# Sparse graph attention: queries and residual rows of all targets in natural order beside the sort, with one gather per tile

## What is computed

```python
hs = layer_norm(x) * ln1_scale + ln1_bias          # sources
ht = layer_norm(h_target) * ln1_scale + ln1_bias   # targets
q, k, v = (ht @ Wq + bq) / sqrt(32), hs @ Wk + bk, hs @ Wv + bv
probs = softmax(where(adj != 0, q @ k.T, -1e30))   # per head
ht = ht + (probs @ v) @ Wo + bo
h2 = layer_norm(ht) * ln2_scale + ln2_bias
out = layer_norm(x + nodemask * (h2 + gelu(h2 @ W1) @ W2))
```

## Time and profile before

| what | value |
|---|---|
| median of the runs | 298.78 us (298.43 to 299.57, 3 runs) |
| span of the profiled execution | 290.6 us |
| time of that execution itself | not shown; the median is 8.2 us over the span |
| PE, VectorE, ACT, POOL busy | 226.5, 211.9, 165.7, 183.8 us |
| moved by DMA | 58.03 MB, 200 GB/s in the mean |

### The profile page before, as it was taken

The page is one execution under the profiler, slowest core; times in us unless marked ns, Lnnn a source line. Parts: engine busy times, 40 slices in busy tenths (PEclk is TensorE's granted clock), DMA queues, the critical chain, the costliest instruction groups (busy, mean ns, idle before and its releaser), DMA issues.

```text
span 290.6 us, 4144 instructions
## 1 busy us (share of the span) xinstructions
PE 226.5 (78%) x1319; PEld 177.8 (61%) x1319; DVE 211.9 (73%) x619; ACT 165.7 (57%) x286; POOL 183.8 (63%) x203
## 2 busy tenths in 40 slices
PE   7499998921124867899889898997799999597990
PEld 7344442300012555898779778996688898496990
DVE  2436999799843885696887869899979997798111
ACT  2598999800003467866866799686376534353420
POOL 8761536860048768787877867878856678047542
PEclk9789999995555699999999999999979999999997
DMA  6999999999975436655555645455662446112120
GB/s 167 357 399 415 417 410 416 406 396 333 365 228 175 147 103 189 187 166 157 153 169 165 177 123 161 136 169 173 187 167 77 121 138 151 38 38 72 36 72 27
DMA packets 23457, 58.03 MB, mean 200 GB/s; under 512 B 4019, under 2 KB 12485, under 8 KB 21382
## 3 DMA queue, kind: packets, MB, share of 16 engines
q0 software_dynamic: 8368, 27.01, 31.8%
q1 hardware_dynamic: 14228, 29.91, 27.3%
q10 hardware_dynamic: 834, 0.79, 1.3%
HBM read 51.40 MB, written 10.49 MB: 213 GB/s over the span
## 4 chain that ended last, share of the span: by engine, by line
POOL 26%; PE 20%; DVE 19%; issue 12%; DMA 11%; ACT 10%; SPq 1%; POOLq 0%; ACTq 0%; DVEq 0%
POOL arena L761 16%; DMA tab_scratch<-in_x_dram 6%; PE bank L1014 6%; PE bank L869 5%; POOL tab L751 4%; PE score L1005 4%; DVE arena L1699 4%; ACT arena L1210 4%; POOL rstd_late L781 4%; DVE arena L1705 3%; DMA arena<-kv_scratch,places 3%; ACT arena L1201 2%; ACT tab L1193 2%; DMA tab<-in_x_dram 2%; DVE arena L1658 2%
## 5 line engine op out<-in xcount | busy, mean ns | idle before, releaser
L761 POOL DMA_INDIRECT arena<-kv_scratch,places x79 | 87.9, 1112 | 22.2 <-issue 22.2
L1005 PE MATMUL score<-h_t,w_sb 128*128 128x128 f32 x512 | 62.3, 275 | 0.0
L1014 PE MATMUL bank<-w_sb,gelu_t 128*128 128x256 f32 x256 | 61.7, 386 | 0.0
L1005 PEld LDWEIGHTS score<-h_t,w_sb 128*128 128x128 f32 x512 | 60.0, 192 | 0.6 <-ACT h_t L1329 0.3
L1014 PEld LDWEIGHTS bank<-w_sb,gelu_t 128*128 128x128 f32 x256 | 47.8, 193 | 5.8
L1275 ACT ACTIVATE gelu_t<-score 128x512 f32<-128x512 f32 x32 | 19.1, 597 | 26.6 <-PE score L1005 26.4
L781 POOL TENSOR_TENSOR rstd_late<-var_late,minus_half 128x1 f32<-128x1 f32 (+3 forms) x23 | 21.0, 912 | 20.7 <-DVE var_late L1768 20.4
L751 POOL DMA_INDIRECT tab<-tab_scratch,places x16 | 17.7, 1109 | 22.5 <-DVE place_value L1628 18.1
L869 PE MATMUL bank<-tab,arena 128*128 128x512 f32 x64 | 30.7, 629 | 1.0 <-ACT arena L1201 0.7
L1658 DVE TENSOR_TENSOR arena<-arena,query 128x1024 f32<-128x1024 f32 (+3 forms) x22 | 24.5, 1113 | 4.4 <-DMA arena<-kv_scratch,places 2.3
L1660 DVE TENSOR_REDUCE logits<-arena 128x32 f32<-128x1024 f32 (+3 forms) x22 | 24.4, 1110 | 0.8
(11 more groups left out here) (148 smaller groups left out, 422.8 us busy)
## 6 DMA issues: line engine op xcount, KB each, us to landing
arena<-in_adj_dram SPq DMA_DIRECT2D x6, 1024.0 KB, 11.4
w_sb<-in_adj_dram SPq DMA_DIRECT2D x6, 1024.0 KB, 12.8
kv_scratch<-arena SPq DMA_DIRECT2D x8, 512.0 KB, 10.3
tab<-in_x_dram SPq DMA_DIRECT2D x4, 512.0 KB, 10.9
own_t<-in_adj_dram SPq DMA_DIRECT2D x2, 1024.0 KB, 11.1
gelu_t<-in_adj_dram SPq DMA_DIRECT2D x2, 1024.0 KB, 10.7
tab_scratch<-in_L_gnn_h_target_dram SPq DMA_DIRECT2D x1, 2048.0 KB, 13.0
tab_scratch<-in_x_dram SPq DMA_DIRECT2D x1, 2048.0 KB, 17.4
```

Of the source, the lines that this page charges most:

```text
L761: pool.indirect_dma_start(kv_ring[:, ring_at[m] + j, :], None, kv_dram[:, :], at).then_inc(gathered[m][piece], 16)
L1005: mm = pe.matmul(hid_ps[(2 * n + half) % 3][:, f % 4 * P:(f % 4 + 1) * P], w1_sb[:, k, f * P:(f + 1) * P], h2_t[:, n % 2, k, :], start=(k ...
L1014: pe.matmul(ff_ps[:, 0:D], gelu_t[:, n % 2, f, :], w2_sb[:, f, :], start=(f == 0), stop=False, skip_group_check=True)
```

## The change

The 2048 targets are treated like the sources, in natural order and before the sort has ended. h_target comes in four chunks of 512 rows (`load_h`) and runs through `unit_stats`, `rsqrt1`, a `normalise` that is now on POOL for chunks 2 to 7 (the last two of x, all of h), `turn_rows` and `copy_turned`. `project_target` makes the queries, `copy_target` takes them out, and `make_residual` on POOL makes the residual row (scale, shift and bo added). `save_table` stores both beside a copy of x in a table of 3 KB rows. After the sort one gather per tile brings x, residual and query; `turn_own`, `project_query`, `normalise_own`, `copy_own`, `copy_query`, the own statistics and `newton` are gone. `project_out` adds the gathered residual with one matmul by the identity. Wq's scaling goes from VectorE to POOL, the hidden layer gets a fourth PSUM bank, `WARM` grows from 32 to 72, and the orders of all engines are written anew. In the diff, parts for the dense path and declarations are left out.

```diff
-    TAB = 2 * D
+    TAB = 3 * D
+    Q_AT = 2 * D
...
+    OWN_AT = [3, 6, 10, 14, 18, 23, 28, 33, 39, 46, 54]
+    ROWS_BY = [(0, 7), (7, 13), (13, 20), (20, 26), (26, 34), (34, 41), (41, 48), (48, 55), (55, 61), (61, 68), (68, 75), (75, 81), (81, 81), (81, 81), (81, 81), (81, 81), (81, 81)]
...
-    WARM = 32
+    WARM = 72
...
+        lead_fetches = [(0, -1), (0, 0), (0, 1), (1, -1), (1, 0), (1, 1), (2, -1), (2, 0), (2, 1), (3, -1), (3, 0), (ROOT, "res"), (3, 1), (3, 2), (4, -1)]
...
+            def save_table(j):
+                sp.wait_ge(query_ready, j + 2)
+                sp.wait_ge(residual_ready, j // CT + 1)
+                sp.dma_start(tab_dram[j * P:(j + 2) * P, D:TAB].rearrange("(i p) n -> p i n", p=P),
+                             table_out[:, j:j + 2, :]).then_inc(table_saved, 16)
...
+            for t in range(0, 12, 2):
+                save_kv(t)
+            sp.dma_start(tab_dram[:, 0:D], x[:, :]).then_inc(rows_copied, 16)
+            save_kv(12)
+            save_kv(14)
+            for j in range(0, TILES, 2):
+                save_table(j)
...
+            def normalise(c):
+                pool.wait_ge(rstd_ready, turn_of[c] + 1)
+                for i in range(CT):
+                    rows = chunk_rows[c][:, i, :]
+                    pool.tensor_scalar(rows, rows, rstd[:, c, i:i + 1], shift[:, c, i:i + 1], ALU.mult,
+                                       ALU.add).then_inc(late_normed, 1)
+            def make_residual(c):
...
+                pool.tensor_tensor(rows, rows, scale_bc.rearrange("p (a n) -> p a n", a=1).to_broadcast([P, CT, D]),
+                                   ALU.mult).then_inc(residual_step, 1)
...
+                pool.wait_ge(coded, QK * (QUARTERS - 1 if k < CHUNKS // 2 else QUARTERS))
+                pool.tensor_tensor(made, rows, shift_bc.rearrange("p (a n) -> p a n", a=1).to_broadcast([P, CT, D]),
+                                   ALU.add).then_inc(residual_ready, 1)
...
             rsqrt1(2)
+            normalise(2)
             rsqrt1(3)
+            normalise(3)
+            pool.tensor_scalar(wq_sb[:, :, :], wq_sb[:, :, :], Q_SCALE, None, ALU.mult).then_inc(wq_scaled, 1)
+            rsqrt1(4)
+            normalise(4)
...
+            rsqrt1(5)
+            normalise(5)
             add_v(0)
-            wait_listing(0)
+            rsqrt1(6)
+            rsqrt1(7)
...
+            normalise(6)
+            normalise(7)
             add_v(1)
...
+            make_residual(4)
             add_v(2)
+            make_residual(5)
             add_v(3)
+            make_residual(6)
+            make_residual(7)
...
                     if m == 0:
-                        pool.wait_ge(rows_copied, 32)
+                        pool.wait_ge(rows_copied, 16)
+                        pool.wait_ge(table_saved, 16 * TILES // 2)
...
+            def project_target(j):
...
+                pe.matmul(proj_ps[t % 2][:, 0:D], ones_bf[:, :], bias_rows[:, :], start=True, stop=False, skip_group_check=True)
+                for k in range(DK):
+                    mm = pe.matmul(proj_ps[t % 2][:, 0:D], rows[:, k, :], wq_sb[:, k, :], start=False, stop=(k == DK - 1),
+                                   skip_group_check=True)
...
+            turn_rows(4)
             make_keys(2)
             project(13)
             project(14)
             project(15)
+            turn_rows(5)
+            project_target(0)
+            project_target(1)
             make_keys(3)
-            project_mean()
+            project_target(2)
+            project_target(3)
+            turn_rows(6)
+            project_target(4)
+            project_target(5)
+            project_target(6)
+            project_target(7)
+            turn_rows(7)
...
             pe.matmul(rank_ps[:, 0:P], class_total[:, :], below[:, :], start=False, stop=True).then_inc(rank_summed, 1)
+            project_target(8)
+            project_mean()
+            for j in range(9, TILES):
+                project_target(j)
...
+                pe.matmul(attn_ps[:, 0:D], ident[:, :], tab_of(n)[:, D:Q_AT], start=True, stop=False, skip_group_check=True)
...
+                for s in range(lo, hi):
+                    if s + 1 < hi:
+                        project_out(s + 1)
+                    mlp_in(s, 0)
+                    mlp_in(s, 1)
+                    mlp_out(s, 0)
+                    if s + 1 < hi:
+                        turn_h2(s + 1)
+                    if lo == 0 and s + 2 < hi:
+                        turn_context(s + 2)
+                    mlp_out(s, 1)
+                    add_h2(s)
...
+                weigh_keys(0, 0, SLOTS[ORDER[0]])
                 sum_tally()
                 weigh_values(0, 0, SLOTS[ORDER[0]])
                 weigh_keys(1, 0, SLOTS[ORDER[1]])
+                take_stats((0, -1), 0, None)
                 set_flag()
                 weigh_values(1, 0, SLOTS[ORDER[1]])
+                make_shift((0, -1))
                 weigh_keys(2, 0, SLOTS[ORDER[2]])
```

559 lines of the change are left out of this document (209 added, 350 removed).

## The result

| | before | after |
|---|---|---|
| median of the runs (lowest to highest) | 298.61 us (297.06 to 299.57) | 322.41 us (320.34 to 326.5) |
| ratio, 95% interval | | 1.0788 [1.0722, 1.0854] |
| span of the profiled execution | 290.6 | 318.6 |
| its own time | not shown | 320.34 |
| first gather F | 82.64 | 104.48 |

A forecast was written before the change was run, and what follows sets the result against it. The loop was taken as bound by PE's matmuls and, close by, POOL's gathers. First gather 14.4 us later, less 7.2 gained from there on, gave +7.2 on 298.8: 306.0 us, range 292 to 317.

The forecast's parts named there:

- What bounds the kernel: Loop: PE's matmuls and POOL's gather stream are two close bounds; the change lightens only the first, 95 gathers stay.
- room: End of the sort: only VectorE works (22.9 of 25.3 us), PE, ACT and POOL idle; not empty for transfers.
- F = 97: Front: first gather at 97 us, 14.4 later than now, through POOL's add_v, the mean, projections, places and last save.
- VectorE: four more chunks of statistics: Front, VectorE: 2.3 us each, 9.1 in all, less 0.4 for wq; 2.6 covered by waits, ranks about 81.
- The lead, F + 21.3 to the power of step 0: First gather to first MLP: first keys at F + 6.5, MLP at F + 20, power of step 0 at F + 21.3.
- The loop, 132.7 us: After the lead to the last gather's end: 81 x 1.41 + 12.8 + 4.4 + 1.3 us, POOL the bound.
- what can be won is POOL's waiting of 7.4 us: Loop: POOL's 7.4 us of waiting for the variance can be won, of which about 1.3 us returns.
- The tail: Last gather's start to last context stays 22.4 us; from there to the end 23.6 plus 2.2 for the new PE order.
- What lies around the span: Outside the profiled span: 8.2 us between the 298.78 us median and the 290.6 us span, kept unchanged.
- Gathers that speed up: Rival, loop: gather spacing falls to 1.26 us, 81 gathers give 12 us, time 293.8; chance 0.22.
- Even, at DMA's floor of 89: Rival, front: cheap POOL, fast clock and quick saves put F at 89 to 91, time 299; chance 0.13.
- A dear tensor_scalar: Rival, front: POOL's tensor_scalar at 1.3 us or more puts F past 107, time 316 or more; chance 0.15.

The follow-up runs named there:

- e14: On e10 (Newton steps on VectorE), POOL again waits for the variance where it waited, only the power left out: 324.42 us, 1.1053 to the kernel before.
- e15: Changed kernel with the step table of the kernel before for VectorE's keys and values: 341.61 us, 1.1605 to the kernel before.
- e17: On e13, all computing of target rows left out, table filled with zeros by POOL, all transfers kept: 311.66 us, 1.0402 to the kernel before.
- e1: Changed kernel with the residual rows left out, POOL writing zeros instead of two wide tensor_tensors: 312.46 us, 1.0528 to the kernel before.
- e3: Changed kernel with 32 warm-up transposes instead of 72: 324.22 us, 1.0824 to the kernel before.
- e5: Changed kernel with each of POOL's eight 1024-wide residual instructions split into four of 256: 318.11 us, 1.0681 to the kernel before.
- e6: Changed kernel with TensorE projecting targets 8 to 15 ahead of the class sums instead of behind them: 313.09 us, 1.0496 to the kernel before.
- e9: Changed kernel with the loads of Wo, W1 and W2 issued before the table saves: 320.85 us, 1.0797 to the kernel before.
- e7: Changed kernel with 110 filler transposes on TensorE between the place matmuls and the first context: 322.64 us, 1.0834 to the kernel before.
- e16: Changed kernel with the own gather bringing 2 KB a row instead of 3, x left out: 319.49 us, 1.0854 to the kernel before.
- e4: Changed kernel with context transposes behind the MLP's second half and the last tile's first values a step earlier: 317.28 us, 1.0618 to the kernel before.
- e11: Changed kernel with the orders of e4, e6 and e9 together: 310.28 us, 1.0338 to the kernel before.
- e13: e11 with the narrow residual pieces of e5: 306.39 us, 1.0434 to the kernel before.
- e10: Changed kernel with late reciprocal roots by Newton steps on VectorE, no power on POOL in the loop: 351.73 us, 1.1821 to the kernel before.

## Why the prediction was right and wrong, point by point

**What bounds the kernel.** Two bounds close together in the loop, of which the change lightens only one: borne out by e14 and e15, though which part of the second binds is open. The row's "room" beside the sort was there for TensorE, but the kernel's orders used 9 us of it for waiting.

**F = 97.** It was 104.5; this step failed first, by its reason. The dear unknown, POOL's tensor_scalar, I took at 0.87 us; it costs 0.60, so add_v(3) ended at 78.4 and not at 82.6: POOL's own sum didn't decide. The wide tensor_tensor I took at 2.0; it costs 2.4. The 72 warm-ups took 9.7 us and not 14, and delayed nothing. The ranks I put at 81; they came at 89.5. Of that, 6.8 us lie between the pick of the last quarter and the ranks (16.9 us instead of 10.1), where I had nothing; the rest lies before the pick, which was 8.1 us late where I had 6.1. Those 6.1 were near by luck: I took them for VectorE's new work, and e17 shows some 5 us without that work. The failed sentence is "VectorE: four more chunks of statistics", which priced VectorE's own new work and gave POOL's 19 us of wide instructions no effect on it. e1 shows the effect on F (8.9 us), e3 and e5 the manner: a held instruction ends with POOL's. The Trainium skill has the rule that I didn't weigh here: "SBUF — State Buffer", section "Who interferes with whom", calls the ports that VectorE and GpSimd share an exclusive lock, held for the whole instruction, against VectorE's copies, casts and tensor_scalars in their fast modes and its instructions with two SBUF inputs, and not against reductions. The traces agree: 1.83 us instead of 0.29 for a tensor_scalar, 0.42 for the reduction beside it; I had used the contention for the loop's gathers alone. Behind the ranks the order of steps was as forecast but for one more projection (target 8) ahead of the mean, the sum too: 15.0 us from ranks to F, where I had 16. e6 shows that this was a choice of order and no need.

**The lead, F + 21.3 to the power of step 0.** It was F + 24.6. I let the first keys start at F + 6.5; they started at F + 8.3, because the weights, which I had noted only as not needed before F, were being loaded beside the first gathers (e9, where they are loaded earlier: F + 6.5). The slow clock of the first output projections wasn't in the sum either; e7 couldn't separate it.

**The loop, 132.7 us.** 137.5 from the same point to the last gather's end. 81 gathers with their gaps took 117.4 where I had 114.2 (both from groups of POOL), the waits 4.0 after the first where I allowed 1.3, the powers 10.6 instead of 12.8 and the stores 5.3 instead of 4.4. The step "what can be won is POOL's waiting of 7.4 us" was too hopeful: these waits come from the other chain. The gathers' part, 3.2 us more, is the larger one, and has no cause shown: a row gather took 1.15 us after 1.13, an own one 1.23 after 1.13, and not for its third KB (e16). TensorE was busy 120.5 us for them after 125.8, at a granted clock of 0.94 after 0.99. That a relieved TensorE idles, loses clock and so works longer for less is read from these rows and not tested by itself.

**The tail.** From the last gather's start to the end of the last context 25.0 us instead of 22.4, from there to the end 28.2 instead of 25.8. The last tile's first values stand one step later. The mechanism of the second, the transposes ahead of the MLP's half, was in the forecast with 2.2 us; it cost 2.4 us more than that, and the half of the MLP behind the wait ran at half clock (3.62 us instead of 1.89). e4 recovers 3.5 us of the two in its profile.

**What lies around the span.** I kept 8.2 us there, the median less the span of another execution. It is 1.7 us for the changed kernel's profiled execution (320.34 against 318.6). That was luck for the number: the span was missed by 20.8 us (297.8 against 318.6), the time only by 16.4, since this term was 6.5 too large and the median lies 2.1 above the profiled execution.

**The rivals.** Gathers that speed up: no, 1.15 us a row gather after 1.13. Even, at DMA's floor of 89: there is a floor (e17, near 92 without the weights by the estimate), but the changed kernel never came near it. A dear tensor_scalar: no; a time of this rival's size came from elsewhere. The bound of the range failed because no case held two misses of one sign, before F (7.5 us) and behind it (13.3 us), together.

## What to carry to other kernels

Before moving work to an idle engine, list which instructions of the busy engine run beside it and price them as if they waited for the whole neighbour instruction; keep such neighbours narrow, or away from the serial stretch. Then ask of each engine's order what stands behind the moved work although it doesn't need it: moves of a few lines (targets, turned contexts, last values, weights) gave back about half of this loss (ratio 1.079 to 1.034 in e11, to 1.043 in e13 with narrow pieces). Count, too, the new loads that stand ahead of the old ones in the queue. Work that feeds another engine in order (the statistics for POOL's powers) shouldn't be moved back for the sake of a wait elsewhere, before it is shown that this wait costs anything.

## What the runs showed of the hardware

- How much a hold costs small instructions: 0.17 becomes 1.81 us for 128x16, 0.23 becomes 2.39 for 128x128, and six in a row went from 1.0 to 9.7 us (e3). MAX8 from PSUM (3.25 us for sixteen) and tensor_reduce (0.42) kept their times beside the same POOL instructions. POOL's fill, which reads nothing, held a tensor_scalar too: `capped` took 0.43 us instead of 0.17 and ended at 81.09, 0.04 behind the fill (e1).
- A POOL tensor_scalar with two operations and per-partition operands takes 0.60 us for 128x256, less than the 0.73 to 0.76 of an add of two tensors; 1024-wide tensor_tensors with a broadcast operand take 2.35 to 2.44.
- In one execution of 384.6 us, unbroken gathers on POOL, 1.25 us apart, came with stretches of 5 to 10 us in which nearly all other engines stood (e10); e14, where POOL waited now and then, shows none. The cause is open.
- A table save of 512 KB landed 2.7 to 3.1 us after its issue where the queue was empty (the last four of the changed kernel, from 94.6 us on), and 7.6 to 10.4 us after it in a full one (e17).
